# Graph network block on one Trainium2 core: the second convolution in float32r, two strips per product

## What is computed

```python
def _L0_gnn_ref(x, edge_index, W1, b1, W2, b2):        # two convolutions
    h = relu(gcn_conv(x, edge_index, W1, b1))
    return gcn_conv(h, edge_index, W2, b2)
# gcn_conv: h = x @ W; out[dst] += h[src] * dinv[src] * dinv[dst], self loops too; + b
def _L1_gnn_ref(x, edge_ids, edge_attr, W1, b1, W2, b2):
    msg = relu(concatenate((x[row], edge_attr)) @ W1 + b1)
    agg = segment_sum(msg, col, n) / maximum(cnt, 1)
    return relu(concatenate((x, agg)) @ W2 + b2)
h = maximum(layernorm(x), 0);  x = x + _L0_gnn_ref(h, ...)
h = maximum(layernorm(x), 0);  x = x + _L1_gnn_ref(h, ...)
```

## Time and profile before

| what | value |
|---|---|
| median of the runs | 3397.44 us (3390.28 to 3404.46) |
| span of the profiled execution | 3499.7 us |
| the same, above the median | 102.3 us |
| mean granted TensorE clock | 0.890 |
| PE / weight loads / DVE / ACT / POOL busy | 78% / 62% / 45% / 31% / 54% |
| 1400 to 2000 us, PE / POOL / DVE / ACT busy | 466 / 256 / 20 / 1 us |

### The profile page before, as it was taken

One profiled execution on the slowest core, in us unless ns is written; L12 is line 12 of the kernel. 1 busy time (PEld: TensorE's weight loads), 2 busy tenths in 40 slices (PEclk: granted clock), 3 DMA queues, 4 the chain that ended last, 5 costly groups with the idle time before them and its releaser, 6 DMA issues.

```text
span 3499.7 us, 54147 instructions
## 1 busy us (share of the span) xinstructions
PE 2746.7 (78%) x18926; PEld 2159.2 (62%) x18927; DVE 1592.3 (45%) x3094; ACT 1071.7 (31%) x3149; POOL 1876.6 (54%) x1751
## 2 busy tenths in 40 slices
PE   2755697889947765787878647998998989888987
PEld 0114486777736654565656536777777777777766
DVE  7988985766623433000000253444444444444436
ACT  6504234556625533000000012333333333333321
POOL 3750767778866732534445134565565555555660
PEclk9995989999968977878888768999999999999989
DMA  9012122323322323433434232323233233332321
GB/s 358 28 35 76 34 83 96 130 98 128 147 85 94 133 97 97 159 124 132 163 125 163 91 98 69 94 90 101 90 95 92 86 104 92 89 92 88 105 73 45
DMA packets 127284, 365.86 MB, mean 105 GB/s; under 512 B 36226, under 2 KB 79591, under 8 KB 120599
## 3 DMA queue, kind: packets, MB, share of 16 engines
q10 hardware_dynamic: 21792, 186.56, 13.8%
q0 software_dynamic: 58928, 89.45, 10.0%
q1 hardware_dynamic: 46377, 87.47, 7.1%
HBM read 230.80 MB, written 132.55 MB: 104 GB/s over the span
## 4 chain that ended last, share of the span: by engine, by line
PE 62%; DVE 11%; issue 10%; another core or an unknown queue 8%; ACT 3%; POOL 2%; DMA 1%; ACTq 1%; DVEq 0%; SPq 0%; POOLq 0%
PE ps_feat L920 12%; PE ps_node L920 11%; PE ps_extra L1069 7%; PE ps_sum L1032 4%; PE pre_banks L908 3%; PE pre_banks L1023 3%; PE ps_feat L1057 3%; PE ps_feat L1053 3%; PE ps_sum L1053 2%; PE ps_sum L1057 2%; PE ps_node L1053 2%; PE ps_node L1057 2%; POOL region_b L705 2%; DVE region_c L1757 2%
## 5 line engine op out<-in xcount | busy, mean ns | idle before, releaser
L680 POOL DMA_INDIRECT permuted<-rows_or_lows,slot_of_edge x768 | 871.7, 1135 | 528.3 <-DVE agg L1766 222.9
L662 POOL DMA_INDIRECT rows<-table,region_a x800 | 786.5, 983 | 685.7 <-issue 210.5
L920 PE MATMUL ps_feat<-region_a,region_b 128*128 128x256 bf16 x3528 | 506.9, 290 | 71.4 <-issue 70.8
L920 PE MATMUL ps_node<-region_a,region_b 128*128 128x256 bf16 x3528 | 513.6, 290 | 60.6 <-issue 57.6
L920 PEld LDWEIGHTS ps_feat<-region_a,region_b 128*128 128x128 bf16 x3528 | 359.3, 103 | 156.5 <-issue 97.4
L920 PEld LDWEIGHTS ps_node<-region_a,region_b 128*128 128x128 bf16 x3528 | 358.2, 103 | 148.7 <-issue 86.9
L1069 PE MATMUL ps_extra<-region_b 128*128 128x128 f32 x2352 | 335.0, 284 | 86.4 <-ACT region_b L1299 48.0
L1069 PEld LDWEIGHTS ps_extra<-region_b 128*128 128x128 f32 x2352 | 302.0, 199 | 92.6 <-issue 72.1
L1757 DVE TENSOR_TENSOR region_c<-iota_key,region_c 128x1568 bf16<-128x1568 f16 (+1 forms) x324 | 353.2, 1090 | 0.0
L1933 DVE TENSOR_TENSOR region_b<-consts,region_a 128x512 f32<-128x512 f32 x336 | 208.2, 620 | 186.9 <-PE ps_extra L1069 97.6
L1928 DVE TENSOR_SCALAR region_b<-rows_or_lows,consts 128x512 f32<-128x512 bf16 x336 | 159.8, 479 | 288.8 <-remote 133.1
(11 more groups left out here) (263 smaller groups left out, 4534.9 us busy)
## 6 DMA issues: line engine op xcount, KB each, us to landing
counts<-region_a ACTq DMA_DIRECT2D x24, 3136.0 KB
region_a<-counts ACTq DMA_DIRECT2D x22, 3136.0 KB
rows_or_lows<-block_lows ACTq DMA_DIRECT2D x72, 448.0 KB
permuted<-region_b SPq DMA_DIRECT2D x25, 833.0 KB
region_a<-permuted SPq DMA_DIRECT2D x24, 833.0 KB
rows_or_lows<-edge_cols_in POOLq DMA_DIRECT2D x24, 544.0 KB
region_a<-attr_t_in SPq DMA_DIRECT2D x50, 256.0 KB
rows<-table,region_a POOLq DMA_INDIRECT x800
```

Of the source, the lines that this page charges most:

```text
L662: nc.gpsimd.indirect_dma_start(rows[:, s, j * D:(j + 1) * D], None, tables[2], bass.IndirectOffsetOnAxis(ap=message_rows[:, c * TC + j:c * ...
L680: nc.gpsimd.indirect_dma_start(permuted, bass.IndirectOffsetOnAxis(ap=slot_of_edge[:, r * RT + k:r * RT + k + 1], axis=0), edge_rows_of[:, ...
L920: ins = mm(strip_bank(buf), parts[:, h, k], counts[buf][:, h], start=(h == 0 and k == 0), stop=(h == SB - 1 and k == PARTS - 1), skip_grou ...
```

## The change

It touches the second convolution and the table split of the node phase before it.

- The table is held as two float32r parts (`halves`): ACT copies the value, DVE subtracts the copy. `part` and `rests` do this once per group for n = 1.
- The counts stay bf16 in HBM and in `region_a` (`count_pair`, two strips side by side). Before use they are widened to float32r, in pieces of 2 blocks by 2 strips (25 per pair, the last of one block), into one of 4 slots (`wide`). DVE widens the even pieces, ACT the odd ones.
- PE multiplies one part of one block with both strips at once: 512 columns, 2 x 49 = 98 products per pair, 12 pairs, each in one bank.
- DVE adds 512 columns at once for each pair, between its casts of the next pair.
- ACT loads the next pair by halves of the blocks, 24 and 25, each when all pieces of that half are widened.
- POOL's pace is counted in pairs; the gathered turn stands after pair 2. Some semaphores are merged.

```diff
+halves = beside("table_halves", [P, SB, 2, D], F32R)
+wide = beside("wide_counts", [P, WIDE_SLOTS, WIDE_BLOCKS, 2, STRIP], F32R)
+count_pair = region_a[:].bitcast(BF16).rearrange("p (s h d) -> p s h d", s=2, h=SB)
+WIDE_BLOCKS = 2
+STRIP_PAIRS = STRIPS // 2
+WIDE_SLOTS = 4
+FIRST_PIECES = 12
+STRIP_ADDED_AT = 4
-TURN_AFTER_APPLIED = {4: 0}
+TURN_AFTER_APPLIED = {2: 0}

+        def widen(engine, k, p):
+            a, b = PIECES[p]
+            at = k * len(PIECES) + p
+            if p in (0, 1) and k:
+                engine.wait_ge(C["loaded_a"], k * 16)
+            if p in (FIRST_PIECES, FIRST_PIECES + 1) and k:
+                engine.wait_ge(C["loaded_b"], k * 16)
+            if at >= WIDE_SLOTS:
+                engine.wait_ge(consumed, at - WIDE_SLOTS + 1)
+            to, of = wide[:, at % WIDE_SLOTS, 0:b - a], count_pair[:, :, a:b].rearrange("p s h d -> p h s d")
+            if WIDENED_BY[p] == "act":
+                nc.scalar.activation(to, of, ACT.Copy).then_inc(widened["act"], 1)
+            else:
+                nc.vector.tensor_copy(to, of).then_inc(widened["dve"], 1)

 # POOL
-strip = i * STRIPS // (SLOTS * TC + PACED[1] * RT)
-pool.wait_ge(strip_added[strip % 2], STRIPS // 2 + strip // 2 + 1)
+pair = i * STRIP_PAIRS // (SLOTS * TC + PACED[1] * RT)
+pool.wait_ge(strip_added[pair % 2], STRIPS // 2 + pair // 2 + 1)

 # PE
+            def apply_wide(k, p):
+                a, b = PIECES[p]
+                slot = (k * len(PIECES) + p) % WIDE_SLOTS
+                engine = WIDENED_BY[p]
+                pe.wait_ge(widened[engine], widened_upto(k, p + 1, engine))
+                for h in range(a, b):
+                    for j in range(2):
+                        ins = mm((ps_feat if k % 2 else ps_node)[:, 0:2 * STRIP], halves[:, h, j],
+                                 wide[:, slot, h - a].rearrange("p s d -> p (s d)"), start=(h == 0 and j == 0),
+                                 stop=(h == SB - 1 and j == 1), skip_group_check=True)
+                ins.then_inc(consumed, 1)
-                    for k in range(STRIPS):
...
-                        for h in range(SB):
-                            apply(buf, h)
+                    for k in range(STRIP_PAIRS):
+                        pe.wait_ge(strip_added[k % 2], k // 2 + (STRIPS // 2 + 1))
+                        for p in range(len(PIECES)):
+                            apply_wide(k, p)

 # ACT
+                    if n:
+                        hold(G["tab"], k + 1)
+                        blocks = blocks_of(g)
+                        nc.scalar.activation(halves[:, blocks, 0], tab[g % 2][:, 0:blocks.stop - blocks.start], ACT.Copy).then_inc(G["part"], 1)
+                        return
+            def load_pair(k, half):
+                pieces = len(PIECES) if half else FIRST_PIECES
+                a, b = (PIECES[FIRST_PIECES][0], SB) if half else (0, PIECES[FIRST_PIECES][0])
+                for engine in ("dve", "act"):
+                    act.wait_ge(widened[engine], widened_upto(k, pieces, engine))
+                if k:
+                    act.wait_ge(C["loaded_" + "ab"[half]], k * 16)
+                act.dma_start(count_pair[:, :, a:b].rearrange("p s h d -> p s (h d)"),
+                              counts_dram[2 * k:2 * k + 2, :, a * STRIP:b * STRIP].rearrange("s p c -> p s c")
+                              ).then_inc(C["loaded_" + "ab"[half]], 16)
-                    with act.Fori(1, STRIPS // 2) as use:
...
+                    for k in range(STRIP_PAIRS):
+                        for p in range(len(PIECES)):
+                            if WIDENED_BY[p] == "act":
+                                widen(act, k, p)
+                            if k + 1 < STRIP_PAIRS and p == FIRST_PIECES:
+                                load_pair(k, 0)
+                        if k + 1 < STRIP_PAIRS:
+                            load_pair(k, 1)

 # DVE
+                    if n:
+                        blocks = blocks_of(g)
+                        dve.wait_ge(G["part"], parts_upto(n, g + 1))
+                        v.tensor_tensor(halves[:, blocks, 1], tab[g % 2][:, 0:blocks.stop - blocks.start], halves[:, blocks, 0].bitcast(F32),
+                                        ALU.subtract).then_inc(G["rest"], 1)
+                        return
+            def add_applied(k):
+                dve.wait_ge(consumed, (k + 1) * len(PIECES))
+                add_bank((2 * k - 2) % STRIPS, k % 2, 2 * STRIP)
-                    for k in range(STRIPS):
-                        use, buf = k // 2, k % 2
-                        add_strip((k - 2) % STRIPS, buf, use + (STRIPS // 2 + 1))
+                    for k in range(STRIP_PAIRS):
+                        for p in range(len(PIECES)):
+                            if k and p == STRIP_ADDED_AT:
+                                add_applied(k - 1)
+                            if WIDENED_BY[p] == "dve":
+                                widen(dve, k, p)
+                    add_applied(STRIP_PAIRS - 1)
```

More of the change, by code:

```diff
@@ L6 @@
 F32 = mybir.dt.float32
+F32R = mybir.dt.float32r
 BF16 = mybir.dt.bfloat16
@@ L103 @@
 PARTS = 3
+WIDE_BLOCKS = 2
+STRIP_PAIRS = STRIPS // 2
+WIDE_SLOTS = 4
+PIECES = [(a, min(a + WIDE_BLOCKS, SB)) for a in range(0, SB, WIDE_BLOCKS)]
+FIRST_PIECES = 12
+WIDENED_BY = ["dve" if p % 2 == 0 else "act" for p in range(len(PIECES))]
+STRIP_ADDED_AT = 4
 MASKED = -1048576.0
@@ L1189, in node_phase @@
                         own_columns(done)
-                        part(done, 1)
+                        if n == 0:
+                            part(done, 1)
                     if g + 1 + n < NG:
                         features(g + 1 + n)
-                    if done >= 0:
+                    if done >= 0 and n == 0:
                         part(done, 2)
@@ L1684, in node_phase @@
                 if n < 2:
-                    dve.wait_ge(G["part"], NG * PARTS * (n + 1))
+                    dve.wait_ge(G["part"], parts_upto(n, NG))
             def edge_turn(e, i, first, messages=False):
```

73 lines of the change are left out of this document (39 added, 34 removed).

## The result

The changed kernel takes 3318.4 us (median of 4 runs, 3309.1 to 3325.9) where the kernel before took 3401.0 beside it (4 runs, 3390.3 to 3413.8): ratio 0.9756, 95% interval 0.972 to 0.979, so 82.6 us less. The forecast was 242 less: the change gives a third of that, though 3318 lies just inside the range. The profiled execution of the changed kernel is the run of 3309.1 us, its span 3307.3.

What follows compares the result with a forecast made beforehand. PE, working alone in the second convolution with issue idle time and low clock, was taken as the bound. Afterwards POOL's end (1350 + 411) decides: 1762 for 2055, 293 us less, minus 51 for the profile: 242 less, 3155 us; range 3070 to 3320.

Steps and rivals of the forecast that it cites:

- Products 218 ns, one pass: Second convolution: 1176 products of 512 columns at 218 ns each, 21.4 us a pair, 257 us for 12 pairs.
- Half rate: Rival, second convolution: 430 ns a product, PE done at 1893, 86 us less, 3311 to 3360 us; chance 0.04.
- float32 speed: Rival, second convolution: float32r executed as float32, 0.86 us a product, 419 us more, about 3816 us; chance 0.08.
- Casts hidden: Second convolution: widening takes DVE 9.6 to 15 us and ACT 12.6 per pair, under PE's 21.4, costing nothing.
- A: Follow-up theory, second convolution: while POOL issues indirect DMAs one behind the other, other engines' issue and hand-overs slow down.
- Start of the stage: Second convolution: PE begins at 1341, 12 us earlier, because the node phase before it drops part copies.
- Hole under the gathers 25: Second convolution: PE loses 25 us under POOL's gathers; with pairs 257 and turn 21, done at 1644.
- POOL 411 us, and POOL decides: Second convolution: POOL's unheld gathers and scatters take 411 us, ending at 1761, later than PE's path at 1720; chance 0.40.
- The runs: half of 102 us taken off: Whole kernel: median of runs is 102 us under the profiled span; half deducted, 242 us less instead of 293.
- issue idle time remains: Rival, second convolution: PE still issues slowly while POOL issues, done at 1796; 183 us less, about 3240 us; chance 0.22.
- the idle time isn't in the runs: Rival, second convolution: in the runs it ended some 210 us earlier already; 83 us less, 3314 us; chance 0.08.
- POOL is blocked by the casts: Rival, second convolution: 156 DVE casts add their whole 0.68 us to POOL; 234 us less, about 3213 us; chance 0.15.

Runs made afterwards that it cites:

- the later group: Both kernels timed again, unchanged: the kernel before 3493.7 us, the changed kernel 3334.6 us.

## Why the prediction came out as it did

- **Products 218 ns, one pass.** Right, nearly: 227 measured, 22.2 us a pair against 21.4. Half rate and float32 speed are out.
- **Casts hidden.** Right in length (DVE 0.72 us on average, 0.69 undisturbed; ACT 1.06) and, without A, in effect: PE then waits 14 us for casts, 12.7 of them for DVE's at the start.
- **Loads hidden.** Right: with the scatters held, the pairs follow each other at 22.2 us, and no cast that waits for a load keeps PE waiting.
- **Start of the stage.** The sum let PE start when the node phase lets it. Missed: the first cast stands on DVE behind the wait for the aggregate's store, where the old products needed no DVE. 11 us on the slow place, 12.8 on the quick, where removing it gained nothing. So the 12 us that the node phase was to give came out as 1.4. PE started at 1332.9, ahead of the summed 1341, only because the first convolution had ended 18 us earlier.
- **"Hole under the gathers 25", hence PE done at 1644: the step that failed.** I read the hole of the earlier trace rows as one that belongs to the 32 gathers and goes away with them, though the strips of the earlier trace rows showed it beside scatters too and POOL was about to issue without its strip waits. It belongs to every burst. PE ended at 1827 after 495 us instead of 303, and the nearly two hundred us lost are A's: 489 us with the scatters, 309 without. On the quick place the stage took 301 us against the summed 303, by luck: the hole of 25 wasn't there, and the pairs (267 us in place of 257) and the turn with the waits for its gathers and the slow first products (34 in place of 21) took its room.
- **POOL 411 us, and POOL decides.** The size was nearly right: from PE's start to the last scatter 430 us on the quick place (363 bare, 20 for the casts, 40 for 32 scatters left over from the first convolution), 456 on the slow one with 70 of waits. The sum had "they aren't held at all"; on the slow place they were, since the pairs didn't come at 21 us. That it decides is right only on the quick place.
- **The runs: half of 102 us taken off.** Wrong by size. Between the two profiled executions the span fell by 192 us, near the 183 of the rival "issue idle time remains", whose mechanism this is. The nearness is luck: the node phase and the convolution gave 133, and 60 came from stages that the change doesn't touch. (In that rival 396 us at 5.3 records per us are 2099 records, not 2040, which would make it 190; and the low end of the range, 3397 less 335, is 3062, not 3070.) Between the runs it fell by 83, exactly the number of the rival "the idle time isn't in the runs". Its mechanism is not shown, though: the changed kernel's profiled execution is one of its runs, holes and all. What differs is the kernel before, 3401 in the runs of the result and 3494 in the later group, where the change is worth 159 us (ratio 0.956, 0.949 to 0.964). Its profiled execution, 3500, is like the later group. How slow the slow place is varies, and more for the kernel before; nothing in one trace would have told me.
- **"POOL is blocked by the casts."** Right in kind, a quarter to a fifth in size: I summed whole casts, 106 us; 17 to 25 were measured. The Trainium skill, "SBUF — State Buffer", section "Who interferes with whom", has the one that comes second wait for the whole of the other's instruction, where DVE is in a two-port mode. The rows agree that DVE's casts hold POOL up (1121 ns a scatter beside one, 960 without), but not by the whole of each, 0.69 us. The same section has PE and ACT wait for nobody at those ports; on the slow place both idle some 10 us a piece beside POOL's DMAs, so whatever A is, by that rule it isn't the ports.

The account in one sentence: the change took the products of a pair of strips from 32.1 to 22.2 us, with all else 115 us of PE's path on the quick place; 54 of these are hidden behind POOL, and on the slow place POOL's DMAs stretch the shorter stage too, from some 300 us to 495.

## What to carry to other kernels

Idle time put down to issue, with no semaphore behind it, is worth a look at what another engine does at that moment: here the holes of PE begin some time after a burst of POOL's indirect DMAs begins (8 to 10 us in the kernel before, 17 to 33 in the changed one) and end some us after it. The changed kernel issues as many of these DMAs in the stage as the old one, 288, in 6 bursts of 24 to 72 instead of 23 of mostly 12. Before a faster stage is credited, the engine that runs beside it must be summed to its end: on the quick place that one line (363 us of DMAs at 1.26 us) gives most of what is left of the gain. A match of two spans should be taken apart by stage before a mechanism is credited with it: here a third of the difference lay in stages that nobody had changed. And a version should be timed in more than one place: moving scatters and the turn made 2738 of 2765 us in one and gained nothing in the other (3369 against 3335, with fewer DVE casts besides).

## What the runs showed of the hardware

- The same program, the kernel before, took 2825 us in four groups of runs and 3400 to 3494 in others. Under it POOL's indirect DMAs, 1.26 us apart in both, slow PE, DVE and ACT on the slow place (pieces of the changed kernel 6 to 12 us apart, single old products up to 2 us apart) and not on the quick one: 256 of them cost 178 us, 0.7 us each. A stage without them takes the same on both (node phase 85.1 and 85.4 us).
- In a hole of PE on the slow place no instruction packet moved for 40 us (1370 to 1410) while PE started four pieces: the instructions were there.
- A float32r product of 512 columns goes at 227 ns, the float32 one of the earlier trace rows at 860.
- A DVE cast to float32r beside a scatter of POOL lengthens it from 960 to 1121 ns on average; a cast of ACT doesn't (959).
- How far POOL has come by the end of the first convolution varies by some 13 us between executions of one program, and so does its last scatter (1562.0 and 1575.4). On the slow place the messages of one and the same program part take 1386 to 1447 us.
